# A selective scan worked by units of both channel halves instead of one, with two channel products moved between engines

## What is computed

```python
da = jnp.exp(dt[..., None] * a)              # a = -exp(a_log)
db = (dt * u)[..., None] * b[:, :, None, :]
def step(h, inp):
    da_t, db_t, c_t = inp
    h = da_t * h + db_t
    y = jnp.einsum('bds,bs->bd', h, c_t)
    return (h, y)
_, ys = jax.lax.scan(step, h0, ...)
y = ys.transpose(1, 0, 2) + u * d            # then y * silu(z), projected out
```

## Time and profile before

| | us |
|---|---|
| median of 3 runs | 1235.8 (1233.55 to 1248.97) |
| the profiled execution | 1227.98 |
| its span in the trace | 1226.1 |
| of it, this block and its hand-over | from 848.5 to about 1050.5 |

### The profile page before, as it was taken

How to read it: one execution, slowest core, us unless ns; L and a number is a source line. 1 busy time by engine, 2 the same in 40 slices (tenths; PEclk the granted TensorE clock), 3 DMA queues, 4 the chain that set the end, 5 groups by cost and what they waited for, 6 DMA issues and landing times. The chain is left out here.

```text
span 1226.1 us, 22767 instructions
## 1 busy us (share of the span) xinstructions
PE 1023.5 (83%) x8317; PEld 743.5 (61%) x8317; DVE 992.2 (81%) x1983; ACT 719.6 (59%) x1522; POOL 600.8 (49%) x899
## 2 busy tenths in 40 slices
PE   5889998476699999999999798690888888768697
PEld 3555654154699999999998566430333333546555
DVE  5999999746699888988886537679999999667575
ACT  3676865055466666666664263375777777247454
POOL 4600000012898888888884231101799999225361
PEclk9598989688899999999999979795899999869989
DMA  3000000020311122112100010002000000000001
GB/s 75 1 1 2 1 2 1 1 102 13 136 49 63 69 76 74 64 68 76 74 4 1 1 24 1 1 1 66 1 0 1 1 1 1 1 1 3 2 0 31
DMA packets 18767, 33.39 MB, mean 27 GB/s; under 512 B 5200, under 2 KB 13888, under 8 KB 18656
## 3 DMA queue, kind: packets, MB, share of 16 engines
q1 hardware_dynamic: 16768, 30.89, 7.3%
q10 hardware_dynamic: 1888, 1.05, 0.4%
HBM read 31.02 MB, written 0.92 MB: 26 GB/s over the span
## 5 line engine op out<-in xcount | busy, mean ns | idle before, releaser
L2259 POOL TENSOR_TENSOR m_h_in<-m_dtu,m_bs 128x448 f32<-128x448 f32 x128 | 144.4, 1148 | 70.7 <-DVE m_dtu L2303 53.6
L777 DVE SCALAR_TENSOR_TENSOR l0r_u<-l0r_u,l0r_a_col 128x1024 f32<-128x1024 f32 x110 | 136.0, 1276 | 5.5 <-ACT l0r_u L687 5.4
L2326 DVE TENSOR_TENSOR_SCAN m_hs<-msp_da,m_h_in 128x448 f32<-128x448 f32 x128 | 136.0, 1079 | 2.5 <-ACT msp_da L2286 1.7
L1158 POOL TENSOR_TENSOR bl_sc<-bl_sc,bl_topall 125x1456 f32<-125x1456 f32 x32 | 105.2, 3289 | 59.6 <-ACT bl_topall L1320 59.6
L687 ACT ACTIVATE l0r_u<-l0r_pu 128x512 f32<-128x512 f32 x216 | 108.6, 638 | 31.8 <-PE l0r_pu L589 31.2
L2222 PE MATMUL msp_py<-m_hc,ident 128*128 128x448 f32 x256 | 118.2, 546 | 0.0
L589 PE MATMUL l0r_pu<-l0r_xs,l0r_eb 32*128 32x256 f32 x896 | 107.4, 468 | 7.3 <-ACT l0r_u L687 4.8
L1395 PE MATMUL bl_pS<-b_qw,bl_xcT 128*125 128x112 f32 x768 | 104.0, 278 | 0.0
L589 PEld LDWEIGHTS l0r_pu<-l0r_xs,l0r_eb 32*128 32x128 f32 x896 | 74.6, 214 | 38.9 <-ACT l0r_u L687 28.2
L870 POOL MEMSET bq_lT<- 128x256 f32 x1 | 0.3, 311 | 196.7 <-POOLq L505 196.7
L2277 ACT ACTIVATE m_bs<-msp_pb 128x448 f32<-128x448 f32 x128 | 69.2, 541 | 45.3 <-PE msp_pb L2206 43.8
(11 more groups left out here) (392 smaller groups left out, 2536.8 us busy)
## 6 DMA issues: line engine op xcount, KB each, us to landing
b_xc<-in_ctx SPq DMA_DIRECT2D x16, 750.0 KB
bl_more<-in_ctx SPq DMA_DIRECT2D x16, 750.0 KB
x_tm<-in_x SPq DMA_DIRECT2D x1, 896.0 KB, 6.2
cw_cT<-in_ctx_headT SPq DMA_DIRECT2D x1, 896.0 KB, 4.5
out_dram<-x_tm SPq DMA_DIRECT2D x4, 224.0 KB, 2.5
l0r_xr<-in_x ACTq DMA_DIRECT2D x4, 192.0 KB, 5.4
w_up<-in_L_ffn_w SPq DMA_DIRECT2D x1, 512.0 KB, 4.1
w_down<-in_L_ffn_w SPq DMA_DIRECT2D x1, 512.0 KB, 5.3
```

The lines of the kernel that those rows point to most:

```text
L777: ve.scalar_tensor_tensor(state(c, i, r), prev, a_col[:, :], state(c, i, r), ALU.mult, ALU.add).then_inc(s["step"], 1)
L1158: pool.tensor_tensor(sc[0:KP, n % 3, :, :], sc[0:KP, n % 3, :, :], over(topall[0:KP, n % 2, :].unsqueeze(1), [KP, KT + 1, QR]), ALU.subtra ...
L2259: pool.tensor_tensor(h_in[:, n % NU, :], dtu[:, half, cols], bs[:, n % NU, :], ALU.mult).then_inc(s["db"], 1)
L2326: ve.tensor_tensor_scan(hs[:, n % NU, :], da[:, n % 2, 0:CH], h_in[:, n % NU, :], 0.0, ALU.mult, ALU.add).then_inc(s["scan"], 1)
```

## The change

A unit now is one state of both halves of a chunk: 64 units with scans, products and `h_in` of 896 columns. The b and c rows are spread and copied once per unit instead of once per half. The decays stay two ACT instructions of 440 columns per unit, into a `da` that has two buffers of 1024 columns; to make room in PSUM `pb` and `pc` have one buffer each (before: two). `py` has one buffer per half, where before it had two that alternated. Buffers: `h_in` 4, `hs` 7, `hc` 3, `bs` 4, and POOL's products have their own tile `hcp` with 2, a semaphore of their own, and are summed five units behind (`DEFER`) instead of three. POOL owns four units of 16 (1, 4, 7, 10) instead of three. `dtu` has two buffers: DVE makes that of the first chunk, POOL the other three, at state 14. `dtu` keeps dt's sign, and `skip` subtracts. The last `gated` is split between POOL and DVE. ACT copies c one unit later than before.

```diff
-        NU = 6
-        h_in = sb("h_in", [P, NU, CH])
-        hs = sb("hs", [P, NU, CH])
-        hc = sb("hc", [P, NU, CH])
-        bs = sb("bs", [P, NU, CH])
+        NI, NS, NV, NB = 4, 7, 3, 4
+        h_in = sb("h_in", [P, NI, H2, CH])
+        hs = sb("hs", [P, NS, H2, CH])
+        hc = sb("hc", [P, NV, H2, CH])
+        hcp = sb("hcp", [P, 2, H2, CH])
+        bs = sb("bs", [P, NB, CH])
-        UNITS = NC * H2 * DS
+        UNITS = NC * DS
-        OWN, AHEAD = (3, 8, 13), 3
+        OWN, AHEAD, DEFER = (1, 4, 7, 10), 3, 5
-            pb, pc = psum2("pb", [P, 2, 512]), psum2("pc", [P, 2, 512])
-            da = psum2("da", [P, 2, 512])
-            py = psum2("py", [P, 2, 512])
+            pb, pc = psum2("pb", [P, 512]), psum2("pc", [P, 512])
+            da = psum2("da", [P, 2, 1024])
+            py = psum2("py", [P, H2, 512])
...
                 def wide_c(n):
-                    if n >= 2:
-                        row_read(pe, n - 2)
+                    if n:
+                        row_read(pe, n - 1)
...
                 for n in range(UNITS + 3):
+                    if n >= 3 and n - 3 not in owned:
+                        add(n - 3)
                     if n + 3 < UNITS:
                         wide_b(n + 3)
-                    if n + 1 < UNITS:
-                        wide_c(n + 1)
-                    if n >= 3:
-                        add(n - 3)
+                    if n - DEFER in owned:
+                        add(n - DEFER)
+                    if n < UNITS:
+                        wide_c(n)
...
             @block.gpsimd
+                for n in range(UNITS + AHEAD):
+                    k, st = n // DS, n % DS
+                    if n < UNITS:
+                        if st == 0:
+                            pool.wait_ge(s["dtu"], k + 1)
+                        pool.wait_ge(s["bcopied"], n + 1)
+                        if n >= NI:
+                            pool.wait_ge(s["scan"], n - NI + 1)
+                        pool.tensor_tensor(h_in[:, n % NI, :, :], dtu[:, k % 2, :, :], both_halves(bs[:, n % NB, :]),
+                                           ALU.mult).then_inc(s["db"], 1)
                     if n - AHEAD in owned:
                         readout(n - AHEAD)
+                    if st == 14 and k + 1 < NC:
...
+                        pool.tensor_tensor(dtu[:, (k + 1) % 2, :, :], dt[:, :, span(k + 1)], u[:, :, span(k + 1)],
+                                           ALU.mult).then_inc(s["dtu"], 1)
+                    if st == 6 and 0 < k < NC:
+                        gated(k - 1)
...
             @block.scalar
+                    for half in range(H2):
+                        act.activation(da[:, n % 2, half * CH:(half + 1) * CH].rearrange("p (b t) -> p b t", t=L)[:, :, 1:L],
...
                     if n + 2 < UNITS:
                         copy_b(n + 2)
-                    if n in owned:
+                    if n - 1 in owned:
+                        copy_c(n - 1)
...
             @block.vector
-                for g in range(UNITS // DS):
-                    _, half, _, cols = unit(g * DS)
-                    ve.scalar_tensor_tensor(dtu[:, half, cols], dt[:, half, cols], -1.0, u[:, half, cols], ALU.mult,
-                                            ALU.mult).then_inc(s["dtu"], 1)
+                ve.tensor_tensor(dtu[:, 0, :, :], dt[:, :, span(0)], u[:, :, span(0)], ALU.mult).then_inc(s["dtu"], 1)
```

## The result

| | before | after |
|---|---|---|
| median of 20 runs, us | 1234.7 | 1223.8 |
| lowest and highest | 1229.6 to 1252.7 | 1221.5 to 1242.4 |
| the profiled execution / its span | 1227.98 / 1226.1 | 1223.22 / 1221.4 |

The ratio is 0.9931, with a 95% interval of 0.9913 to 0.9949: 8.5 us less (6.3 to 10.7), where 8 were forecast. Some executions of both kernels (two of 20 after, four of 20 before) take some 15 to 19 us longer, and the ratio leaves them out; the medians of all 20 differ by 10.9 us. The forecast of 1228 us was 8 less than a median of three runs, 1235.8; the median is 1223.8, 4.2 us under it. So the difference was met more closely than the number. The change is within the 2% to which the forecast gave 91%.

What follows compares the result with a forecast made beforehand. DVE sets the pace before; after, POOL is at least an equal bound. Last product 12.3 us earlier, less 4 for the clock and 0.3 at the end: 8 less than 1235.8, so 1228 us, range 1213 to 1241.

Steps and rivals of the forecast that it cites:

- DVE's durations: DVE in the block: scans of 896 columns start 1.93 us apart, products take 1.00; together 175.1 us.
- The start: Block start: seven dtu instructions leave DVE, so the first scan comes 4.6 us earlier, at about 852.4.
- ACT's new wait: ACT's copy of c ahead of the decays holds the scan 0.3 us per owned unit: 4.3 to 4.8 us.
- POOL: POOL in the block: 86 instructions of 2.08 us, 178.9 us; last `h_in` ends at 1030.0, last product 1033.0.
- At least an equal bound: POOL ends at 1033.0, nearly together with DVE and ACT's waits at 1032.0; 1 us more gives 1034.
- The clock: PE idles about 2.4 us in every 8.3 in the owned region: about seven clock falls, costing 4 us.
- 0.6 us each: What one clock fall costs DVE through a delayed row c: 1.7 us of PE lag, less the slack.
- The end: Last product to projection: 4.5 us, with sums 1.6, two skips, gated halves and hand-over; 0.3 more than before.
- (a): Rival: the clock holds and buffers suffice; 12 to 19 us less, 1217 to 1224; chance 20%.
- (b): Rival: POOL does not gain from length, 2.27 us an instruction; 3 to 8 us slower, 1239 to 1244; 8%.
- (c): Rival: PE's clock stays low, 61 us lost if it lasted; half way 1235 to 1255; chance 10%.
- (d): Rival: nothing gained, as waits on `pc`, `hc` and `hcp` buffers take DVE's savings; 1232 to 1239; 17%.

Runs made afterwards that it cites:

- x4: Kernel before, with only POOL making all of `dtu` but the first half chunk: 1231.3 us, ratio to before 1.0007.
- x2: Kernel after, with ACT copying c behind the next decays instead of ahead of them: 1220.1 us, ratio to before 0.9916.
- x9: Kernel after, with sums three behind, the copy of c behind the decays and the last sums drawn forward: 1218.5 us, ratio to before 0.9903.
- x11: x9 without POOL's three gated products within the block: 1217.3 us, ratio to before 0.9813.
- x6: Kernel after, with POOL owning three units of 16 (1, 6, 11) and sums three behind: 1223.5 us, ratio to before 0.9934.
- x5: Kernel after, with POOL's products summed three units behind instead of five: 1218.9 us, ratio to before 0.9892.
- x1: Kernel after, with POOL's products summed six units behind instead of five: 1224.4 us, ratio to before 0.9954.
- x3: Kernel after, with POOL owning three units of 16 (1, 6, 11), sums still five behind: 1237.4 us, ratio to before 1.0041.
- x7: Kernel after, with the last sums drawn forward so only the last stands behind the last product: 1224.0 us, ratio to before 0.9939.

## Why the prediction was right, point by point

**DVE's durations: right.** The 896-column scan shows 2.018 us a record, within the 1.96 to 2.08 named; the distance of starts is 1.93 (927.50 to 929.43). The product shows 1.067 us and the next start 0.98 us later (929.43 to 930.41), where 1.00 was taken. That `da` crosses a PSUM bank, priced at nothing, cost at most 0.03 us a scan, the distance of 1.93 from the forecast's lower bound of 1.90. The product, which reads its one row twice, crosses none.

**The start: right.** 3.6 us to the first scan, 3.5 forecast. As x4 shows, it does not come through whole: 5.5 us at the start of the kernel before became 3.0 at the last product, in the trace.

**ACT's new wait: right in mechanism and in size, for 13 units of 16.** The forecast counts distances of starts, and by these a held unit comes 0.26 us late (2.19 for 1.93) where 0.3 was forecast. As idle time it is 0.17. Thirteen of the 16 owned units show it, 2.7 us idle; three more waits, 0.8 us, belong to falls of the clock. So the 3.5 us idle for 4.3 to 4.8 forecast are nearly the same thing once the lost overlap of some 0.09 us is added to each. x2 took the wait away by the reordering that the forecast's mechanism implies. That only 0.9 us came back belongs to the next point.

**POOL: the sum right, what follows it wrong in part.** A record is 2.088 us (forecast 2.08), a start every 2.04 (five in 10.22 us), and never 1.69 or 2.27. Here the forecast multiplied records where for DVE it had multiplied distances; 86 x 2.04 is 3.4 us less, and 3.0 us of waits for row b, of which it had 1, make up for most of it. The forecast has the last `h_in` end 1030.0 - 848.9 = 181.1 us after the first row b:

```profile
853.04 10.22 POOL L2264 TENSOR_TENSOR m_h_in<-m_dtu,m_bs 128x896 f32<-128x896 f32 x5 [52.78 <-ACT m_bs L2285]
...
1027.84 4.14 POOL L2264 TENSOR_TENSOR m_h_in<-m_dtu,m_bs 128x896 f32<-128x896 f32 x2
```

It ends at 1031.98, which is 180.3. But the last product ends 7.0 us later (1039.02), not 3.0. The last scan starts 2.1 us behind the last `h_in` (1034.13 in the trace), since a chunk's last five units are all DVE's, at 2.91 us each against POOL's 2.04. Two products follow the last scan and not one, 1.0 us more, because a unit's product stands behind the next unit's scan. And the last product waits for row c, 0.9 us with the lost overlap. The forecast had none of the three. Where one unit in three is owned, POOL needs 4 x 2.04 = 8.2 us for three units and DVE 3 x 1.93 + 2 x 0.98 = 7.8. The bound alternates within a chunk; that was given 1 us in the forecast. "At least an equal bound" holds in x9, as x11 shows; in the kernel after, POOL is never idle for long but nearly always ahead of the scan, and x2 shows only that it stands close behind.

The Trainium skill (GPSIMD Engine Reference, Elementwise — side-by-side cycle accounting) led to an estimate of 1.94 us for POOL's instruction; the trace has 2.09 us a record and 2.04 from start to start, so it does not agree, and the measurement decides. Its advice to leave elementwise work to VectorE was weighed by taking one product in four back: x6 comes out 1.0 us behind x5 in the trace, and 1223.5 against 1218.9 by medians, with overlapping intervals. So sharing helps here by a little, or does not hurt.

**The clock: right that it falls and how often, wrong in what it costs.** Eight falls where seven were forecast, at gaps of 2.2 to 2.4 us where 2.4 was forecast. The count has some luck in it: the forecast had a gap in every 8.3 us of the owned regions and a fall in at most every second one; there were nine such gaps past 870 us, and eight went with a fall. The term was 4 us; what came back in x5, where the clock never fell there, is 2.1, and that also has the order of the sums in it. x1, with over half of the lost clock back, gained 0.7. The step that failed is "0.6 us each". In this order a fall shows as a few tenths: the waits for PE above, 2.6 us, of which x5 has 0.5 too, and the three for ACT, 0.8. The sums slowed by it mostly have room until the next gap. That is a matter of the order and not of falls as such: in x3, with two sums ahead of the row c that ACT copies, falls went with waits of 1.2 to 2.5 us. The Trainium skill (TensorE: Matmul & The Clock Gate, HAM oscillation) describes such repeated falls, there between waits for DMA; the trace agrees on the falls (1.00, 0.79, 1.00 in three stretches of 8 us), and here PE waits for DVE.

**The end: mis-sized.** The term "sums 1.6" was one unit's sums; the trace has three units', 4.67 us, and the skip waits 3.4 us for them. I had read off what comes after the last product in the data and not what stands ahead of the last sum in PE's order. x7 shows 4.5, which was the forecast for a queue in good order.

**The total.** The clock's 4 us were 1.8 more than the last product came late (2.2), and the end was 1.5 too short (6.0 for 4.5). These cancel, so the block was right to 0.3 us, and the difference by the ratio to 0.5, for reasons that were right to 2: the closeness is luck. Within DVE's own sum the rest closes as well: 3.6 at the start + 175.1 = 178.7, and 187.3 were measured. Of the 8.6 between them, the waits of the rows above account for 6.1 (ACT 3.5, PE's rows c 1.7 and 0.9), and of the rest, 2.5 us, some 1.8 is that each of 20 instructions that waited loses the 0.09 us by which it would have overlapped the one before it. The trace shows this once above (2.19 = 1.93 + 0.09 + 0.17); for the others it is an estimate from that. No run changes the length of the units alone, so what it is worth is read from these distances and not from a run.

**The rivals.** (a) fell in the kernel after, since the clock did not hold, though the median, 1223.8, lies in its 1217 to 1224 and not in the forecast's 1224 to 1232. x5 and x9 are what (a) looks like: the clock at 1.00 and 0.99, ratios of 0.9892 and 0.9903, 13 and 12 us less, at the small end of its 12 to 19. (b) is excluded by 2.088 us. (c) did not come in the kernel after; x3 is what it looks like, 0.84 with row c behind two sums, at 1.0041. (d) is excluded by the interval.

## What to carry to other kernels

Cost a hand-written order by what stands ahead of an instruction in its engine's queue, not only by its data: both costly places here were sums in front of something that another engine waited for, the last unit's sum at the end and row c in x3. When one stall is taken away and little comes back, look for the engine that is busy without a pause in the same windows (here GpSimd, at 8.00 of 8), and take work from it alone to see whether it bounds, as x11 does. Spreading the sums evenly over the steps kept TensorE's clock up and needed no later sums; one step a chunk without a sum (x1) was enough for a fall in each of three chunks.

## What the runs showed of the hardware that was not expected

- GpSimd's instructions overlap too: a record of 2.088 us, but a start every 2.04 (five in 10.22 us).
- What a fall of TensorE's clock costs depended on the order behind it. In the kernel after, eight falls (mean granted clock 0.91) and the order that made them cost 2.1 us together in the trace, against x5. In x3, where slowed sums stood ahead of a row that ACT and so DVE waited for, falls went with waits of 1.2 to 1.3 us (low for about 3.4 us) and 2.4 to 2.5 us (low for about 6.8).
- GpSimd kept its 2.07 to 2.12 us an instruction while DVE was busy for 96% of the same stretch, and took 2.08 us for one that ran mostly while DVE was idle (x3, 941.14). A scan took 2.02 us beside GpSimd (927.50) and with GpSimd idle (1034.13). So no slowing of one by the other is seen.
